# Attention layer on one Trainium2 core: the projection streams the image over four column groups, with block transposes on VectorE and the sums of squares on TensorE

## What is computed

```python
x1 = (x - mean_c(x)) / sqrt(var_c(x) + 1e-5) * ln_w + ln_b      # over the 16 channels
out1 = dwconv(x1, 1x7) + dwconv(x1, 1x11) + dwconv(x1, 1x21)    # along w
out2 = dwconv(x1, 7x1) + dwconv(x1, 11x1) + dwconv(x1, 21x1)    # along h
out1 = proj(out1); out2 = proj(out2)                            # 16x16 channel mix and a bias
k1 = v1 = split_h(out1); q1 = split_h(out2)                     # 8 heads of 2 channels
k2 = v2 = split_w(out2); q2 = split_w(out1)
q1, k1, q2, k2 = [t / max(norm(t, axis=-1), 1e-12) for t in (q1, k1, q2, k2)]
out3 = softmax(q1 @ k1.T) @ v1 + q1
out4 = softmax(q2 @ k2.T) @ v2 + q2
y = proj(merge_h(out3)) + proj(merge_w(out4)) + x
```

## Time and profile before

| what | value |
|---|---|
| median of 3 runs | 543.1 us (542.53 to 543.5) |
| span of the profiled execution | 539.1 us |
| PE busy | 466.5 us (87%) |
| DVE busy | 384.9 us (71%) |
| ACT busy | 268.1 us (50%) |
| projection matmuls, L445, PE busy | 53.3 us |
| row sums, L489, DVE busy | 20.6 us |

### The profile page before, as it was taken

One profiled execution on the slowest core, in us unless ns is written; L12 is line 12 of the kernel. 1 busy time (PEld: TensorE's weight loads), 2 busy tenths in 40 slices (PEclk: granted clock), 3 DMA queues, 4 the chain that ended last, 5 costly groups with the idle time before them and its releaser, 6 DMA issues. The chain is left out here.

```text
span 539.1 us, 19085 instructions
## 1 busy us (share of the span) xinstructions
PE 466.5 (87%) x8416; PEld 384.6 (71%) x8416; DVE 384.9 (71%) x625; ACT 268.1 (50%) x366; POOL 44.3 (8%) x64
## 2 busy tenths in 40 slices
PE   4587999985999999978999999749987899999970
PEld 2286999983988898744877778638754587777860
DVE  2794677976888623357899999754833799999962
ACT  2574422424333120027888887730104888888861
POOL 3410000000000000041000040000012000000000
PEclk9889999995999999969999999978996999999995
DMA  8700000000000000000000000000000000000005
GB/s 182 165 1 1 2 2 2 2 1 1 2 3 1 2 1 1 1 0 2 3 4 4 0 0 3 4 2 1 0 0 2 1 4 4 2 0 1 4 4 156
DMA packets 8017, 7.76 MB, mean 14 GB/s; under 512 B 5488, under 2 KB 6800, under 8 KB 7952
## 3 DMA queue, kind: packets, MB, share of 16 engines
q1 hardware_dynamic: 6928, 6.51, 5.0%
q10 hardware_dynamic: 1024, 0.28, 0.3%
HBM read 4.67 MB, written 2.11 MB: 13 GB/s over the span
## 5 line engine op out<-in xcount | busy, mean ns | idle before, releaser
L1068 DVE TENSOR_TENSOR g_wgt<-g_exponents,ps 128x1024 f32<-128x1024 f32 x128 | 151.1, 1206 | 5.1 <-PE ps L913 4.8
L1012 ACT ACTIVATE g_wgt<-g_wgt 128x1024 f32<-128x1024 f32 x128 | 132.2, 1061 | 18.4 <-DVE g_wgt L1068 17.6
L913 PE MATMUL ps<-ident,g_scl 128*128 128x128 f32 x512 | 80.3, 287 | 3.8 <-DVE g_scl L1059 3.6
L928 PEld LDWEIGHTS ps<-g_wgt,g_xt 128*32 128x32 f32 x4096 | 61.6, 111 | 24.0 <-issue 20.9
L928 PE MATMUL ps<-g_wgt,g_xt 128*32 128x64 f32 x4096 | 72.4, 222 | 4.9 <-issue 4.8
L913 PEld LDWEIGHTS ps<-ident,g_scl 128*128 128x128 f32 x512 | 57.4, 141 | 16.6 <-DVE g_scl L1059 4.9
L445 PE MATMUL ps<-projblk,conv_img 128*64 128x64 f32 x1024 | 53.3, 266 | 0.7 <-DVE xcol L495 0.6
L445 PEld LDWEIGHTS ps<-projblk,conv_img 128*64 128x64 f32 x1024 | 52.7, 195 | 1.2 <-DVE xcol L495 1.1
L996 ACT ACTIVATE g_hid<-ps,vec 128x512 f32<-128x512 f32 x32 | 22.0, 688 | 57.0 <-PE ps L872 57.0
L1313 PE MATMUL ps<-high,wb 128*128 128x512 f32 x72 | 30.3, 421 | 5.3 <-DVE rest L1342 5.3
L1313 PE MATMUL ps<-rest,wb 128*128 128x512 f32 x72 | 30.0, 417 | 0.0
(11 more groups left out here) (159 smaller groups left out, 719.4 us busy)
## 6 DMA issues: line engine op xcount, KB each, us to landing
x<-in_x SPq DMA_DIRECT2D x8, 256.0 KB, 6.5
out<-g_result SPq DMA_DIRECT2D x8, 256.0 KB, 4.0
windows<-band SPq DMA_DIRECT2D x4, 256.0 KB, 4.4
c_weight<-in_c_weight SPq DMA_DIRECT2D x1, 576.0 KB, 4.1
g_w<-in_g_w SPq DMA_DIRECT2D x2, 128.0 KB, 2.7
g_gband<-in_g_gband SPq DMA_DIRECT2D x2, 64.0 KB, 2.8
centre<-in_centre SPq DMA_DIRECT2D x1, 64.0 KB, 2.2
ident<-in_ident ACTq DMA_DIRECT2D x1, 64.0 KB
```

The costliest lines, as they stand in the source:

```text
L913: tr = pe.transpose(ps[:, u % 4, P * k:P * k + P], spread(scl[s][:, k, u:u + 1], [P, P]), ident[:])
L928: mm = pe.matmul(ps[32 * j:32 * j + 32, O_BANK, 64 * cb:64 * cb + 64], xt[(s + t) % 2][:, cb, b, :], wgt[s][b][:, t, cb, :], start=(t == 0 ...
L1012: act.activation(w, w, ACT.Exp).then_inc(weight, 1)
L1068: dve.tensor_tensor(wgt[s][u][:], spread(gband[:].unsqueeze(2), shape), spread(s_in, shape), ALU.mult).then_inc(logit, 1)
```

## The change

The projection is turned round. `projblk` becomes the stationary operand in pieces of 32 columns, and the image is the moving one. A job is now four matmuls of 512 moving columns, a strip of 16 lines by one half (32 pixels) of each, which write four groups of 32 partitions of one bank: `cp` by the two halves of the line. A strip is streamed twice, once for each half of the batch (`late`), so there are still eight jobs for each tensor. The result has planes in the partitions. ScalarE adds the bias while it moves the job to SBUF (`biased`, four buffers), and VectorE transposes it in blocks of 32 x 32 into the tensor.

The squares of a tensor go to a buffer of eight heads, three on VectorE and five on ScalarE, between the strips of the next tensor. Their sums are matmuls with a one-hot matrix of 32 columns as the stationary operand, which add up over all four tensors in PSUM bank 6: four after the fourth strip job and four after the eighth of the next tensor, and eight at the end. Then VectorE copies the bank, four transposes turn it, and bound, root and reciprocal follow as before. The order of the tensors stays; only their places in the norms change. In `l0_norm` one small matmul and one copy make the bias, and the constants `onehot` (128 x 256) and `bias_rhs` (49 x 128) take the place of `pair` (128 x 128) and `bias_rhs` (49 x 16).

```diff
-            for t in range(2):
-                mm = pe.matmul(ps[:, 4, C * t:C * t + C], spread(bias_lhs[:, t:t + 1], [nb, P]),
-                               bias_rhs[:], start=True, stop=True)
-            mm.then_inc(bias_mm, 1)
+            pe.matmul(ps[:, 4, 0:2], bias_rhs[:], bias_lhs[:], start=True, stop=True).then_inc(bias_mm, 1)
...
+            def norm_sums(i, half):
+                heads = range(4 * half, 4 * half + 4)
+                pe.wait_ge(squared_v, len(ON_VECTOR) * i + sum(m <= heads[-1] for m in ON_VECTOR))
+                pe.wait_ge(squared_s, (HEADS - len(ON_VECTOR)) * i + sum(m not in ON_VECTOR for m in range(heads[-1] + 1)))
+                for m in heads:
+                    q = 32 * (m % 4)
+                    mm = pe.matmul(ps[q:q + 32, SUM_BANK, :], onehot[:, 2 * TENSORS[i][1] + half, :], sqs[:, m, :],
+                                   start=(i == 0 and half == 0), stop=(i == 3 and half == 1))
+                mm.then_inc(summed, 1)
             for i, (_, _, t, inner) in enumerate(TENSORS):
                 planes = img[t][:] if inner == 0 else img[t][:].rearrange("p h w -> p w h")
                 for g in range(CHUNKS):
...
-                        pe.wait_ge(proj_out, j - 3)
+                        pe.wait_ge(proj_biased, j - 3)
...
-                    for hh in range(ROWS):
-                        for cp in range(CP):
-                            mm = pe.matmul(ps[64 * cp:64 * cp + 64, j % 4, 64 * hh:64 * hh + 64],
-                                           planes[:, ROWS * g + hh], projblk[:, 64 * cp:64 * cp + 64],
+                    strip, late = divmod(g, 2)
+                    for cp in range(CP):
+                        for side in range(2):
+                            q = 64 * cp + 32 * side
+                            mm = pe.matmul(ps[q:q + 32, j % 4, :],
+                                           projblk[:, 64 * cp + 32 * late:64 * cp + 32 * late + 32],
+                                           planes[:, STRIP * strip:STRIP * strip + STRIP, 32 * side:32 * side + 32],
                                            start=True, stop=True)
                     mm.then_inc(proj_mm, 1)
-            pe.wait_ge(summed, 4 * HEADS)
-            pe.matmul(ps[:, NORM_BANK, 0:4 * HEADS * B], pair[:], ssum[:].rearrange("p t m b -> p (t m b)"),
-                      start=True, stop=True).then_inc(nsq_mm, 1)
+                    if i > 0 and g % 4 == 3:
+                        norm_sums(i - 1, g // 4)
+            for half in range(2):
+                norm_sums(3, half)
+            pe.wait_ge(sums_out, 1)
+            for k in range(4):
+                tr = pe.transpose(ps[:, NORM_BANK, P * k:P * k + P], sums[:, P * k:P * k + P], ident[:])
+            tr.then_inc(nsq_mm, 1)
...
+            def act_square(i, m):
+                act.wait_ge(proj_out, CHUNKS * (i + 1))
+                if i > 0:
+                    act.wait_ge(summed, 2 * (i - 1) + m // 4 + 1)
+                act.activation(sqs[:, m, :], TENSORS[i][0][:, m].rearrange("p b h -> p (b h)"),
+                               ACT.Square).then_inc(squared_s, 1)
...
+            for i, (_, _, t, _) in enumerate(TENSORS):
+                for g in range(CHUNKS):
+                    j = CHUNKS * i + g
+                    act.wait_ge(proj_mm, j + 1)
+                    if j >= 4:
+                        act.wait_ge(proj_out, j - 3)
+                    act.activation(biased[:, j % 4, :], ps[:, j % 4, :], ACT.Identity, bias=beta[:, t:t + 1],
+                                   scale=1.0).then_inc(proj_biased, 1)
+                    if i > 0 and g not in ON_VECTOR:
+                        act_square(i - 1, g)
...
-                    dve.tensor_tensor(dst[:, :, :, ROWS * g:ROWS * g + ROWS].rearrange("p m b h -> p h m b"),
-                                      ps[:, g % 4, :].rearrange("p (h b m) -> p h m b", h=ROWS, b=B),
-                                      spread(beta[:, t, :].unsqueeze(1).unsqueeze(3), [P, ROWS, HEADS, B]),
-                                      ALU.add).then_inc(proj_out, 1)
-                    if i > 0:
-                        row_sums(i - 1, g)
-            for m in range(HEADS):
-                row_sums(3, m)
+                    dve.wait_ge(proj_biased, j + 1)
+                    dve.transpose(dst[:, :, HALF * late:HALF * late + HALF, STRIP * strip:STRIP * strip + STRIP]
+                                  .rearrange("p m b h -> p h b m"),
+                                  biased[:, j % 4, :].rearrange("p (h b m) -> p h b m", h=STRIP, b=HALF))\
+                        .then_inc(proj_out, 1)
+                    if i > 0 and g in ON_VECTOR:
+                        dve_square(i - 1, g)
+            for m in ON_VECTOR:
+                dve_square(3, m)
+            dve.wait_ge(summed, 2 * len(TENSORS))
+            dve.tensor_copy(sums[:], ps[:, SUM_BANK, :]).then_inc(sums_out, 1)
```

More of the change, by code:

```diff
@@ L105, in build @@
                 l0_norm(nc, sem, lambda n, s: sb(ln, n, s), d, ident, vec, pad_a, ps, x0,
-                        xrow, xcol, toep, pair, beta, projblk, const_in, later, band)
+                        xrow, xcol, toep, onehot, beta, projblk, const_in, later, band)
             o1c = sb(l0, "o1c", [P, HEADS, B, W])
@@ L109, in build @@
             with ExitStack() as cv:
-                l0_conv(nc, sem, lambda n, s: sb(cv, n, s), ident, pair, ps, xrow, xcol, toep, projblk,
+                l0_conv(nc, sem, lambda n, s: sb(cv, n, s), ident, onehot, ps, xrow, xcol, toep, projblk,
                         beta, o1c, o2r, rn)
@@ L138, in turned_view, with l0_norm @@
     return lay[:].rearrange("p n b h -> p (n b h)").rearrange("p (m i) -> p m i", i=32)
-def l0_norm(nc, sem, sb, d, ident, vec, pad_a, ps, x0, xrow, xcol, toep, pair, beta,
+def l0_norm(nc, sem, sb, d, ident, vec, pad_a, ps, x0, xrow, xcol, toep, onehot, beta,
             projblk, const_in, later, band):
@@ L359, in _, with l0_conv @@
                     dve.tensor_copy(turned_out(lay, g), turned_in(g)).then_inc(evac_v, 1)
-def l0_conv(nc, sem, sb, ident, pair, ps, xrow, xcol, toep, projblk, beta, o1c, o2r, rn):
+def l0_conv(nc, sem, sb, ident, onehot, ps, xrow, xcol, toep, projblk, beta, o1c, o2r, rn):
     img = [sb(f"conv_img{t}", [P, H, W]) for t in range(2)]
-    sqs = sb("sqs", [P, 4, BANK])
-    ssum = sb("ssum", [P, 4, HEADS, B])
+    biased = sb("biased", [P, 4, BANK])
+    sqs = sb("sqs", [P, HEADS, BANK])
+    sums = sb("norm_sums", [P, BANK])
     nsq = sb("nsq", [P, HEADS, 4, HALF])
@@ L397, in l0_conv @@
     JOBS = 2 * CHUNKS
-    TENSORS = ((xrow, 2, 0, 0), (o1c, 1, 0, 1), (xcol, 0, 1, 0), (o2r, 3, 1, 1))
-    NORM_BANK = 7
+    TENSORS = ((xrow, 1, 0, 0), (o1c, 2, 0, 1), (xcol, 3, 1, 0), (o2r, 0, 1, 1))
+    SUM_BANK, NORM_BANK = 6, 7
+    STRIP = 16
+    ON_VECTOR = (2, 5, 7)
     def wait_evacuated(eng, j, on_v, on_s):
@@ L501, in _, with dve_square @@
-            for m in range(HEADS):
-                row_sums(3, m)
+            def dve_square(i, m):
+                if m == ON_VECTOR[0]:
+                    dve.wait_ge(proj_out, CHUNKS * (i + 1))
+                if i > 0:
+                    dve.wait_ge(summed, 2 * (i - 1) + m // 4 + 1)
+                src = TENSORS[i][0][:, m].rearrange("p b h -> p (b h)")
+                dve.tensor_tensor(sqs[:, m, :], src, src, ALU.mult).then_inc(squared_v, 1)
+            for i, (dst, _, _, _) in enumerate(TENSORS):
+                for g in range(CHUNKS):
+                    j = CHUNKS * i + g
+                    strip, late = divmod(g, 2)
+                    dve.wait_ge(proj_biased, j + 1)
[5 more added lines that the diff above has]
+                        dve_square(i - 1, g)
@@ L504, in _ @@
+            for m in ON_VECTOR:
+                dve_square(3, m)
+            dve.wait_ge(summed, 2 * len(TENSORS))
+            dve.tensor_copy(sums[:], ps[:, SUM_BANK, :]).then_inc(sums_out, 1)
             dve.wait_ge(nsq_mm, 1)
-            for odd in range(2):
-                part = slice(64 * odd, 64 * odd + 64)
-                sums = ps[part, NORM_BANK, 0:4 * HEADS * B].rearrange("p (t m k o) -> p o m t k", t=4, m=HEADS, o=2)
-                dve.tensor_scalar(nsq[part], sums[:, odd], L2_EPS_SQ, None, ALU.max).then_inc(nsq_ready, 1)
+            found = ps[:, NORM_BANK, :].rearrange("p (k q r) -> p q k r", k=4, q=4)[:, :, :, 0:8]\
+                .rearrange("p q k (t u) -> p u q t k", u=2)
@@ L509, in _ @@
+            for u in range(2):
+                dve.tensor_scalar(nsq[:, 4 * u:4 * u + 4], found[:, u], L2_EPS_SQ, None, ALU.max).then_inc(nsq_ready, 1)
             dve.wait_ge(norm_ready, 1)
@@ L1434, in shape_constants @@
     mask = (bits[:, :, None] == np.arange(2)).astype(np.float32)
-    pair = np.tile(np.eye(64, dtype=np.float32), (CP, CP))
+    onehot = np.tile(np.eye(8, 32, dtype=np.float32), (P, 1, 1))
     return {"ident": ident, "centre": centre, "meansel": meansel,
```

(2 more changed lines are left out.)

39 lines of the change are left out of this document (15 added, 24 removed).

## The result

The changed kernel takes 557.0 us (median of 4 runs, 552.9 to 560.9), the kernel before 542.8 in the same comparison: a ratio of 1.026, with a 95% interval of 1.019 to 1.033. It is slower, as forecast, but by 14 us in place of 39. The profiled execution spans 551.5 us, 12.4 more than before.

A forecast was written before the change was run, and what follows sets the result against it. The prediction took TensorE's gathering of strided columns in o1c and o2r as the bound. Strips, waits, batches and tail summed to a stage of 102.4 us against 63.8, a span of 577.7 and, with 4.0 added, 581.7 us; range 539 to 598.

The forecast's parts named there:

- What bounds the stage, and that the strided tensors decide: o1c and o2r are bound by TensorE gathering single values from SBUF, 2.34 us a job in o1c before.
- Packed strips at 0.87 us: xrow and xcol: a job is two rounds of four column groups at 0.434 us, 0.87 us in all.
- The strided strip job at 3.85 us: o1c and o2r: a job gathers 4096 single columns at 0.94 ns each, 3.85 us, between 2.75 and 4.70.
- the half us that the sum was said to be good to: The same adding with old durations gave 64.3 us for the old stage of 63.8, so good to half a us.
- a supply that groups share: Strided strips: column groups share one gathering supply; stage 84.8 to 116.0 us, total time 564 to 596 us, chance 0.50.
- The price per group: Strided pair of weight loads: 147 ns for 64 columns, 2.3 ns a column, if each group is slow by itself.
- The second rival: Strided strips: each group slow by itself, no sharing, 2.36 us a job; stage 78.6 us, total 557.9 us; chance 0.17.
- The transpose at 1.04 us: VectorE's 32 transposes take 1.04 us each, like evacuations with scattered writes, with 0.69 and 1.3 as ends.
- Waits before the batches: TensorE waits for squares before the sums: 1.6 us mid-tensor, 2.7 at a tensor's end.
- ScalarE under the strided jobs at 0.69: ScalarE's moves from PSUM and squares take 0.69 to 1.34 us a job, hidden under the strided jobs.
- The clock left at 2.4 GHz: TensorE's new waits are shorter than the old tail's 6.6 us idling, so the clock stays at 2.4 GHz.
- The edits at nothing: Fewer bias instructions and copies against constants larger by 64 + 22 KB: between -0.3 and +0.4 us, taken as 0.

The follow-up runs named there:

- the probe: Changed kernel with extra strided and packed matmul rounds ahead of the projection; at step 64 a round took 0.861 us with one group, 1.105 with four.
- `late_sums`: Changed kernel with each batch of sums issued two strips later, except the batches at the end; 547.6 us, 1.010 of the kernel before.
- `pitch65`: Changed kernel with the images stored at 65 elements a row in place of 64; 549.7 us, 1.013 of the kernel before.
- `packed`: Changed kernel with o1c and o2r reading the image in packed runs, so those tensors come out transposed; 539.2 us, 0.995 of the kernel before.

## Why the prediction was wrong

The direction was right, the size was not: +39 us forecast, +14 measured. Step by step:

- What bounds the stage, and that the strided tensors decide: right. Taking the stride out moves the old stage by 11.4 us and the new one by 18.4.
- Packed strips at 0.87 us: right, they start 0.86 apart.
- The strided strip job at 3.85 us: wrong, and this is the step that failed. It is 2.1 to 2.3 us. With 2.2 in its place the sum falls by 16 x 1.65 = 26.4, from 102.4 to 76.0, against 77.9 measured. That is 1.9 off, not the half us that the sum was said to be good to. The error lay in the sentence that took the jump of the weight loads, from 0.4 ns a column alone to 1.8 with two groups, for a supply that groups share. The rows compared differed in two more things: step 32 against step 64, transposes against matmuls. Nor were the 140 and 194 ns a clean price of a stride: the packed loads of L417, 128 columns too, take 190. One group alone, at the same step, would have settled it, and no row had it; the probe gives 0.861 us for it against 1.105 for four, so four groups share only a small part of what they gather with. That is for moving columns; whether weight loads share wasn't tried. The price per group that the same pair of loads gave, 2.3 ns a column, was nearly right: 1.105 us for 512 columns is 2.16.
- The second rival, groups slow by themselves, gave a stage of 78.6 us and 557.9 for the run; measured were 77.9 and 557.0. Its mechanism is the one that the probe found, but the hit to a us is in part luck: its strip of 2.36 us is somewhat too long, and the stops and the tail, which it took over from the same sum, were too short. It had a chance of 0.17, because a strided load for a transpose passed in 113 ns. That a moving operand behaves as a load of another kind does was an assumption.
- The transpose at 1.04 us: right, medians of 1.05 to 1.12.
- Waits before the batches, 1.6 and 2.7 us by turns, 12.9 in all: right in sum. TensorE idled 13.1 us before the one-hot matmuls, in six stops of 1.4, 2.5, 2.0, 3.3, 1.4 and 2.4. That they lie on the path is shown too: `late_sums` takes 11.0 us off the stage.
- By stretch, from TensorE's starts: xrow and o1c 43.8 forecast, 98.27 - 66.98 = 31.3 measured; xcol 15.7 and 14.4; o2r and tail 42.9 and 32.2. With 2.2 a strip the forecast is 30.6, 15.7 and 29.7: what is left are errors of both signs, and the largest, 2.5 us, is in o2r and the tail.
- ScalarE under the strided jobs at 0.69: missed. Its moves took 912 ns on average and 1729 at the longest. It isn't the bound, but it lengthens the chain from a strip to its square, which TensorE waits for: a strip and its stop were to take 4.7, 5.8 and 4.7 us (with 2.2 a strip) and took 5.0, 6.4 and 6.0, against 4.3, 5.3 and 4.3 in `pitch65`. That the strided reads would slow ScalarE and VectorE was in no term.
- The clock left at 2.4 GHz: not quite, but it cost little. See below.
- The edits at nothing: they cost nothing that shows. The constants did arrive later in one trace, and mending that didn't move the run.

The granted clock in the changed kernel (the third figure from the end; xcol, o2r, tail) was 1.00 in xrow and o1c and then not always:

```profile
99.50:115.50 16.00, 10.64 (x82) 2.86 (x78) 9.77 (x11) 7.36 (x13) 0.00 (x0) 0.92 0.00 1
115.50:137.00 21.50, 17.96 (x66) 4.81 (x58) 10.15 (x11) 12.61 (x14) 0.00 (x0) 0.98 0.00 0
137.00:145.10 8.10, 5.08 (x28) 1.17 (x28) 4.09 (x8) 2.85 (x6) 0.00 (x0) 0.80 0.01 2
```

It was 0.50 (1.2 GHz) from 113 to 116.3 us, after TensorE had idled 3.3 us, and again from 137 to 140.3, after 2.4 us. The first two strided strips of o2r, which fell there, took 2.08 and 2.33 us from start to start, o1c's first two 1.95 and 2.23. In the tail four rounds of sums took 0.8 to 0.85 us in place of 0.43, at most 1.7 us in all, and TensorE waited for squares there too.

The rule of the Trainium skill's "TensorEngine Tiling (Array Packing)", Performance Considerations, holds in full for packed strips only: four groups take 0.429 us a round, as one does, four times the work. At a step of 64 it is four groups in 1.105 against one in 0.861, so tiling still gains 3.1 times; it is the base that is half as fast.

## What to carry to other kernels

Swapping the stationary and the moving operand doesn't remove a stride, it moves it; when a stretch is bound by gathering, make one packed copy on an engine that idles there, or at least take the row pitch off the power of two, which took three lines here and gained 1.4% (0.7 to 2.2%). A batch that one engine does for another belongs some jobs behind the work that it waits for: the same sums cost 11 us less in the stage, 9 in the run, two strips later. Compare structures only with the same mend on both sides. When a sum hangs on whether parallel streams share a supply, look for a row of one stream with the same step before pricing the many.

## What the runs showed of the hardware

- A moving fp32 operand streams at full pace with a step of one or two elements (0.43 and 0.45 us for 512 columns, four groups) and at half pace at steps of 4, 8 and 16 (0.90 to 0.92). One group alone takes 0.43 packed and 0.86 at a step of 64.
- Steps of 32 and 64 elements cost more than that (1.36 and 1.11 us); 65, 66, 68 and 72 don't (0.90 to 0.97). Why 32 is worse than 64 wasn't tried; it ran on for 128 columns before a new start, 64 for 32 columns.
- While TensorE streams at a step of 64, ScalarE's and VectorE's accesses of SBUF take longer: ScalarE's squares 1.03 to 1.83 us against 0.61 in the probe, single squares of both engines 3.6 us in `late_sums`. In the real stage this vanished at 65 (longest move 0.69 us, longest square 0.69).
- A packed strip doubles when the granted clock falls from 1.00 to 0.50 (1.71 us against 0.86 in `packed`, at 89 us); a strided one at 64 hardly changes (2.08 and 2.33 against 1.95 and 2.23).
- VectorE's transpose of 128 x 512 fp32 in 32 x 32 blocks, with every element written apart from its neighbour, takes 1.05 to 1.12 us, as an evacuation with scattered writes does.
